# Attention in two layers: value products on four quarters of TensorE, output in two banks

## The reference

```
part 1: q, k, v = x @ w_q, x @ w_k, x @ w_v         16 heads of 64
        allowed(i, j) = same segment of 64 tokens,
                        or i - j a multiple of 4, not 0, at most 256 away
        out = softmax(q k^T / 8, allowed) v, then @ w_o
part 2: FP4 quantise-dequantise of x and weights, silu(x w_gate) * (x w_up), @ w_down (352 wide)
part 3: a gated recurrence in chunks of 64 tokens, then a silu MLP, 512 wide
part 4: sigmoid(xr W_r) * (relu(xk W_k)^2 W_v)
```

## Time and profile before

| | us |
|---|---|
| median of 3 runs (469.19, 473.04, 474.06) | 473.04 |
| span of the profiled execution, first to last instruction | 468.8 |
| TensorE busy in it (95%) | 444.4 |
| VectorE busy (84%) | 394.0 |
| ScalarE busy (71%) | 333.3 |
| GpSimd busy (63%) | 296.6 |

### The profile page before, as it was taken

How to read it: one execution, slowest core, us unless ns; L and a number is a source line. 1 busy time by engine, 2 the same in 40 slices (tenths; PEclk the granted TensorE clock), 3 DMA queues, 4 the chain that set the end, 5 groups by cost and what they waited for, 6 DMA issues and landing times.

```text
span 468.8 us, 17264 instructions
## 1 busy us (share of the span) xinstructions
PE 444.4 (95%) x6440; PEld 350.0 (75%) x6440; DVE 394.0 (84%) x1344; ACT 333.3 (71%) x975; POOL 296.6 (63%) x491
## 2 busy tenths in 40 slices
PE   7997899999999999999999999998987989999996
PEld 6685688888888888788887778887744757558775
DVE  6885798987888899889887698995899989998775
ACT  3686768868877877886786678695566579987533
POOL 4321488677666858667865588564669897674322
PEclk9999899999999999999999999999999999999999
DMA  7577852346335445344455565364000000000003
GB/s 224 183 246 209 247 142 52 73 99 133 80 74 112 76 79 105 76 85 94 98 108 124 112 124 108 75 125 91 1 1 0 0 2 1 1 0 2 1 0 91
DMA packets 136099, 40.53 MB, mean 86 GB/s; under 512 B 104977, under 2 KB 131025, under 8 KB 136017
## 3 DMA queue, kind: packets, MB, share of 16 engines
q1 hardware_dynamic: 135440, 38.38, 35.7%
q10 hardware_dynamic: 576, 1.05, 0.6%
HBM read 29.44 MB, written 9.96 MB: 84 GB/s over the span
## 4 chain that ended last, share of the span: by engine, by line
PE 59%; POOL 9%; DMA 8%; DVE 8%; ACT 7%; SPq 4%; issue 3%; ACTq 0%; POOLq 0%; DVEq 0%
PE psum L422 10%; PE psum L464 10%; PE psum L484 5%; PE psum L1186 5%; DMA w_rows_dram<-st 4%; PE psum L498 4%; PE psum L495 4%; PE psum L403 4%; PE psum L510 4%; PE psum L1181 3%; PE psum L405 3%; PE psum L404 3%; DMA st<-w_rows_dram 2%; POOL area L1827 2%; ACT pband L569 2%
## 5 line engine op out<-in xcount | busy, mean ns | idle before, releaser
L948 POOL TENSOR_SCALAR pband<-pband,fac 128x192 f32<-128x192 f32 x256 | 103.9, 424 | 80.6 <-DVE fac L771 80.4
L569 ACT ACTIVATE pband<-pband,st 128x192 f32<-128x192 f32 x256 | 113.1, 447 | 1.0 <-DVE st L719 1.0
L719 DVE CUSTOM_DVE_ANT_0 pband<-psum,band_mask 128x192 f32<-128x192 f32 x256 | 76.1, 353 | 0.1
L422 PE MATMUL psum<-keys,q_class 64*64 64x192 f32 (+2 forms) x1536 | 66.2, 274 | 0.0
L464 PEld LDWEIGHTS psum<-ident,pband 128*128 128x128 f32 x384 | 45.4, 141 | 21.4 <-issue 13.3
L422 PEld LDWEIGHTS psum<-keys,q_class 64*64 64x64 f32 x1536 | 57.6, 133 | 1.4 <-issue 1.4
L464 PE MATMUL psum<-ident,pband 128*128 128x128 f32 x384 | 53.0, 273 | 2.2 <-DVE pt L780 2.2
L569 ACT ACTIVATION_READ_ACCUMULATOR pband<-pband,st 128x1 f32 x256 | 49.3, 192 | 0.0
L938 POOL COPY q_class<-q_rows 128x512 f32<-128x512 f32 x32 | 36.5, 1142 | 19.2 <-ACT q_rows L609 19.2
L930 POOL COPY keys<-k_rows 128x512 f32<-128x512 f32 x32 | 36.1, 1130 | 14.0 <-ACT k_rows L601 7.1
L780 DVE COPY pt<-psum 128x512 f32<-128x512 f32 x64 | 43.7, 683 | 0.5
(11 more groups left out here) (213 smaller groups left out, 1090.7 us busy)
## 6 DMA issues: line engine op xcount, KB each, us to landing
v_rows_dram<-arena SPq DMA_DIRECT2D x32, 256.0 KB, 3.4
...
w_rows_dram<-st SPq DMA_DIRECT2D x64, 8.0 KB, 3.0
st<-w_rows_dram SPq DMA_DIRECT2D x64, 8.0 KB, 2.5
...
```

The costliest lines, as they stand in the source:

```text
L422: return pe.matmul(bank[2 * r + head][rows, at:at + y.shape[1]], x, y, start=True, stop=True, skip_group_check=True)
L569: act.activation(x, x, ACT.Exp, bias=mine[:, head:head + 1], scale=-1.0, accum_out=mine[:, 2 + head:3 + head]).then_inc(s_exp, 1)
L719: dve.tensor_tensor_reduce(pband[:, G % P_SLOTS, c, head, :], bank[2 * r + head][:, at:at + BAND], band_mask[:, (0, 1, 1, 2)[w], SEG * (1 ...
L948: pool.tensor_scalar(x, x, fac[:, F % 2, 1, c, head:head + 1], 1.0, ALU.mult, ALU.mult).then_inc(s_scaled, 1)
```

## The change

- **Value products.** The 64 keys of a side or segment product now lie by token half or by class parity, not by head: the rows of the array follow the keys, the columns follow the head, and so products exist for all four quarters. `out_bank` becomes two half banks (256 columns of bank 6 and of bank 7), one for each half of the window's tokens. The side products come in two calls: first those whose keys' rows and bank have the same number, then the crossed ones, after a wait for the first (`s_sides`).
- The products for b = 0 and 1 write two banks too: 16 products of 64 moving columns in place of 8 of 128.
- **Layouts.** `pband`, `pseg`, `v_seg` and `v_side` are laid out anew. The loads of `v_seg` and `v_side` keep their number; their pieces are 128 numbers (512 bytes) in place of 64.
- **Scores.** The same products in another order: for an even class the pair of products of both heads takes the same columns of the array, for an odd class the other ones.
- **Banks.** The query projection writes bank 6, the output product writes `turn_bank[0]` (bank 4). So the next projections wait for `take_out` (`s_out`), the output product waits for the even turn of the next unit to be copied out (`s_pt[0]`), and the turn for b = 0 waits for the sum of two units before (`s_acc`).
- **Order.** TensorE's step is new (below), the output product comes one step earlier, the key projection at the end of the step before. The other engines' steps, the start-up and the rest are put in a new order with the same calls.

```diff
-    s_out, s_mix, s_acc = sem("s_out"), sem("s_mix"), sem("s_acc")
+    s_sides, s_out, s_mix, s_acc = sem("s_sides"), sem("s_out"), sem("s_mix"), sem("s_acc")
 
     bank = [psum[:, k, :] for k in range(8)]
-    turn_bank, out_bank, shared_bank = bank[4:6], bank[6], bank[7]
+    turn_bank, rows_bank, shared_bank = bank[4:6], bank[6], bank[7]
+    out_bank = [bank[6 + half][:, 0:HALF_W] for half in range(2)]
+    query_bank = [shared_bank, bank[6]]
     SEG_AT = 2 * BAND
     CONST = 3
     MASKS = 15
...
     for x in range(1, FIRST_STEP):
         occupants += [(x, "key"), (x - 1, "query")]
-    occupants.append((FIRST_STEP - 1, "query"))
-    for t in range(FIRST_STEP, NS_ALL + 8):
-        occupants += [(t - lag, who) for who, lag in (("key", 0), ("wo", 7), ("query", 0)) if there(t - lag)]
+    occupants += [(FIRST_STEP - 1, "query"), (FIRST_STEP, "key")]
 
     def wait_shared(pe, x, name):
 
+        if (x, name) not in occupants:
+            pe.wait_ge(s_out, x - FIRST_STEP + (name == "query"))
+            return
         at = occupants.index((x, name))
         if at:
             pe.wait_ge(*shared_reader(*occupants[at - 1]))
...
-                    product(0, second, at, x0[:, second], y0[:, SEG:SEG + BAND])
-                    product(1, first, at, x1[:, first], y1[:, 0:BAND])
-                    product(0, first, at, x0[:, first], y0[:, SEG:BAND])
-                    product(1, second, at + SEG, x1[:, second], y1[:, SEG:BAND])
-                    product(0, first, at + P, x0[:, first], y0[:, 0:SEG])
-                    product(1, second, at, x1[:, second], y1[:, BAND:BAND + SEG])
+                    if c % 2 == 0:
+                        product(0, second, at, x0[:, second], y0[:, SEG:SEG + BAND])
+                        product(1, second, at, x1[:, second], y1[:, SEG:SEG + BAND])
+                        product(0, first, at, x0[:, first], y0[:, SEG:BAND])
+                        product(1, first, at, x1[:, first], y1[:, SEG:BAND])
+                        product(0, first, at + P, x0[:, first], y0[:, 0:SEG])
+                        product(1, first, at + P, x1[:, first], y1[:, 0:SEG])
+                    else:
+                        product(0, first, at, x0[:, first], y0[:, 0:BAND])
+                        product(1, first, at, x1[:, first], y1[:, 0:BAND])
+                        product(0, second, at + SEG, x0[:, second], y0[:, SEG:BAND])
+                        product(1, second, at + SEG, x1[:, second], y1[:, SEG:BAND])
+                        product(0, second, at, x0[:, second], y0[:, BAND:BAND + SEG])
+                        product(1, second, at, x1[:, second], y1[:, BAND:BAND + SEG])
...
                 wait(pe, s_pt[odd], e)
+                if b == 0:
+                    wait(pe, s_acc, U - 1)
...
+            def turned(U, b):
+
+                odd, e = b % 2, 2 * U + b // 2
+                pe.wait_ge(s_pt[odd], e + 1)
+                return pt[:, PT_SLOTS * odd + e % PT_SLOTS, :]
+
+            def out_by_class(half):
+                return out_bank[half].rearrange("q (x c) -> q c x", c=DIL)
+
             def weigh(U, b):
+
                 if not there(U):
                     return
                 p, w = divmod(U, NW)
-                odd, e = b % 2, 2 * U + b // 2
                 if b == 0:
+                    pe.wait_ge(s_query, min(U + FIRST_STEP, NS_ALL))
+                    pe.wait_ge(s_key, min(U + FIRST_STEP + 1, NS_ALL))
                     wait(pe, s_out, U)
                     pe.wait_ge(s_v[w], (p + 1) * V_DMAS[w])
-                if b == 2 and w < NW - 1:
-                    pe.wait_ge(s_v[w + 1], (p + 1) * V_DMAS[w + 1])
-                pe.wait_ge(s_pt[odd], e + 1)
-                turned = pt[:, PT_SLOTS * odd + e % PT_SLOTS, :]
-                by_class = out_bank.rearrange("q (x c) -> q c x", c=DIL)
-                for k in range(4):
-                    if b < 2:
-                        c, head = 2 * b + k // 2, k % 2
-                        dims = slice(DH * head, DH * (head + 1))
-                        last = pe.matmul(by_class[dims, c, :], v_both[:, c, w, dims], turned[:, P * k:P * (k + 1)],
-                                         start=(b == 0 and k < 2), stop=False, skip_group_check=True)
-                        continue
+                mine = turned(U, b)
+                for i in range(2):
+                    c = 2 * b + i
                     for half in range(2):
-                        cols = slice(P * k + SEG * half, P * k + SEG * (half + 1))
-                        side = 2 * w + 1 if half else 2 * w - 2
-                        if b == 2 and not 0 <= side < 2 * (NW - 1):
-                            continue
                         for head in range(2):
                             dims = slice(DH * head, DH * (head + 1))
-                            if b == 2:
-                                last = pe.matmul(by_class[dims, k, SEG * half:SEG * (half + 1)], v_side[dims, k, side, :],
-                                                 turned[dims, cols], start=False, stop=False, skip_group_check=True)
-                            else:
-                                last = pe.matmul(out_bank[dims, cols], v_seg[dims, 2 * (TW * w + k) + half, :],
-                                                 turned[dims, cols], start=False, stop=(k == 3 and half == 1),
-                                                 skip_group_check=True)
-                last.then_inc(s_pv[odd], 1)
+                            at = P * (2 * i + head) + SEG * half
+                            last = pe.matmul(out_by_class(half)[dims, c, :], v_both[:, c, w, dims], mine[:, at:at + SEG],
+                                             start=(c == 0), stop=False, skip_group_check=True)
+                last.then_inc(s_pv[b], 1)
+
+            def weigh_segments(U):
+
+                if not there(U):
+                    return
+                w = U % NW
+                mine = turned(U, 3)
+                for j in range(2):
+                    for second in range(2):
+                        for head in range(2):
+                            for half in range(2):
+                                dims, mykeys = slice(DH * head, DH * (head + 1)), slice(SEG * half, SEG * (half + 1))
+                                cols, at = SEG * (2 * j + second), P * (2 * j + head) + SEG * second
+                                last = pe.matmul(out_bank[half][dims, cols:cols + SEG],
+                                                 v_seg[mykeys, HALF_SEGS * w + 2 * j + second, dims],
+                                                 mine[mykeys, at:at + SEG], start=False, stop=False, skip_group_check=True)
+                last.then_inc(s_pv[1], 1)
+
+            def weigh_sides(U, crossed):
+
+
+                if not there(U):
+                    return
+                p, w = divmod(U, NW)
+                if w < NW - 1:
+                    pe.wait_ge(s_v[w + 1], (p + 1) * V_DMAS[w + 1])
+                mine = turned(U, 2)
+                if crossed:
+
+                    pe.wait_ge(s_sides, U + 1)
+                for d in range(2):
+                    for head in range(2):
+                        for odd in range(2):
+                            half = odd ^ crossed
+                            side = 2 * w + 1 if half else 2 * w - 2
+                            if not 0 <= side < 2 * (NW - 1):
+                                continue
+                            dims, mykeys = slice(DH * head, DH * (head + 1)), slice(SEG * odd, SEG * (odd + 1))
+                            at = P * (2 * d + head) + SEG * half
+                            last = pe.matmul(out_by_class(half)[dims, 2 * d + odd, :], v_side[mykeys, d, side, dims],
+                                             mine[mykeys, at:at + SEG], start=False, stop=False, skip_group_check=True)
+                last.then_inc(s_pv[0] if crossed else s_sides, 1)
 
             def output(U):
                 if not there(U):
                     return
                 if U == 0:
                     pe.wait_ge(s_wo, 16)
-                wait_shared(pe, U, "wo")
+                pe.wait_ge(s_pt[0], min(2 * (U + 2), 2 * NS_ALL))
+                wait(pe, s_acc, U)
                 pe.wait_ge(s_out, U + 1)
-                pe.matmul(shared_bank[:, :], wo[:, U // NW, :], o_sb[:, :], start=True, stop=True).then_inc(s_mix, 1)
+                pe.matmul(turn_bank[0][:, :], wo[:, U // NW, :], o_sb[:, :], start=True, stop=True).then_inc(s_mix, 1)
 
             pe.wait_ge(s_con, 2)
             pe.wait_ge(s_const, CONST)
...
             for t in range(FIRST_STEP, DRAIN):
-                project(t, 1)
                 weigh(t - 6, 0)
                 weigh(t - 6, 1)
-                turn(t - 6, 3)
-                output(t - 7)
+                scores(t - 2, 0)
+                weigh_segments(t - 6)
+                weigh_sides(t - 6, 0)
+                scores(t - 2, 1)
+                weigh_sides(t - 6, 1)
```

(23 more changed lines are left out.)

272 lines of the change are left out of this document (140 added, 132 removed).

## The result

| | before | after |
|---|---|---|
| median of the runs, us | 472.1 | 483.2 |
| profiled execution's span | 468.8 | 483.9 |
| first copy into `o_sb` | 66.5 | 69.1 |
| last copy into `o_sb` | 341.9 | 340.4 |
| from it to the end | 126.9 | 143.5 |

The change makes the kernel slower: ratio 1.025, 95% interval 1.020 to 1.031. The forecast was 456 us. The profiled execution of the kernel after is the longest of its four (485.86 us, the others 480.1 to 483.9), so stretches read from its trace are at the upper end.

What follows compares the result with a forecast made beforehand. TensorE, never idle over 20 attention steps of 9.0 us, was taken as the bound. Steps -12.1, late and following steps -0.6 and -1.6, last units -1.5, start-up -1, parts 2 to 4 0: 473.0 - 16.8 = 456.2 us, range 449 to 466.

Steps and rivals of the forecast that it cites:

- parts 2 to 4: The kernel's parts after attention: the same work in another order, put at 0 us (+3 to -3).
- the step as a whole: Each of the 20 attention steps with its waits: 8.4 us, so 168.0 against 180.1, -12.1.
- the late steps: Three steps after the 20, held by statistics round trips and SyncE's queue: -0.6 us; three loop steps after them: -1.6.
- The step of TensorE alone: TensorE's own work in an attention step: middle step 9.27 to 8.30 us, edge step 8.79 to 8.28.
- Rivals 2 and 3: 2: segment products no faster on four quarters, 471 us, chance 0.08; 3: class products keep 54 ns per record, 478, 0.05.
- rival 2: Value products: four quarters not twice as fast, 471 us, chance 0.08; by the 25 ns rule middle step 8.9, about 467.
- The second circle: Attention step: key projection, ScalarE's exponentials, VectorE's factors and even-turn copy, a turn, key projection again: 8.36 us.
- Rival 1: Attention loop: circles of waits between TensorE, ScalarE and VectorE close at 8.75 us, not 8.4: 465 us, chance 0.17.
- The last five units: Five units in the hand-written rest win their value products partly: -1.5 us (0 to -3).
- Start-up: The 66.5 us before the first copy into `o_sb`: one more key projection, fewer packets, -1 us (+1 to -3).
- rival 4: More gain than forecast: late steps follow TensorE, parts 2 to 4 gain 3 us by new order: 449 us, chance 0.06.
- sign that it was wrong altogether: A start-up or a rest that is longer by more than 3 us.

Runs made afterwards that it cites:

- half_products: The changed kernel with half of the side products and half of the segment products left out: 481.9 us, ratio 1.021 to the kernel before.
- best: The changed kernel with the edits of `last_bank` and `rows_on_act` together: 470.1 us, ratio 1.001 to the kernel before.
- last_bank: The changed kernel with parts 2 to 4 in the old order and the last unit's output product in bank 7, not 4: 475.9 us, ratio 1.007.
- rows_on_act: The changed kernel with eleven loads (part 2's rows, plain weights) issued by ScalarE instead of SyncE: 477.7 us, ratio 1.012 to the kernel before.

## Why the prediction was wrong

Three of its terms failed: parts 2 to 4, put at nothing (point 6, over half of the miss), the step as a whole (2) and the late steps (3).

1. *The step of TensorE alone, 8.3.* Right as far as the runs show: segments 14 ns, classes 30 ns apart; without pauses (176.3 - 9.5) / 20 = 8.34. Rivals 2 and 3 are out. (By the rule in rival 2 a middle step comes to 8.30 + 2 x 0.35 = 9.0, not 8.9.) The second circle, put at 8.36, was right too, as `half_products` shows (8.39), so a shorter TensorE step alone would have won nothing more. The rule of the Trainium skill ("TensorE: Matmul & The Clock Gate", "Wait — 56ns, not 53.3ns?"), matmuls never less than about 25 ns apart, doesn't hold for four quarters: the row has 14.
2. *The step as a whole, 8.4.* Wrong, 8.8. The failed step is the sum of TensorE's step from records of a kernel in which no pause occurs: it has no term for the supply of instructions. The change puts 3833 records into 176.3 us where there were 3512 in 180.1, and crowds them, the fastest 124 into 2.2 us instead of 3.1; the seams of the instruction packets then cost 0.48 a step. Rival 1 had the length of the step (8.75), but not the cause: of the waits that it named, the one for `take_out` comes once (1.4 us) and the one for VectorE's copy twice (0.7 us), and taking away the waits for the statistics, or some of VectorE's work, changed nothing.
3. *Late steps and loop steps after them, -2.2.* Wrong, +2.8 in the profiled execution (from -0.3 to +4.6 in the five kernels with the same loop). I had seen SyncE's round of 10.5 us and still counted on some gain. The round is a circle of its own, 10.5 us before and 11.2 after, and doesn't follow TensorE. Eleven issues moved to ScalarE bring 4.2 us (`best` against `last_bank`) to 6.8. A stretch of 6.8 us at the lower clock, which the kernel before doesn't have, adds to the 2.8.
4. *The last five units, -1.5.* Measured -3.1.
5. *Start-up, -1.* Measured +2.6, but it varies from 63.9 to 70.2 in kernels with the same start-up; no cause was tested.
6. *Parts 2 to 4, 0 (±3).* Wrong by 16.6, half of all, and the step that decided the sign. "The same work in another order" was costed at nothing, without a row that shows what an order costs. It costs 11.6 by itself on the old attention. I even counted it as a gain in rival 4. Of the waits that it makes, those for `y(0)` and `hb` were seen; moving `y(0)` won nothing, so which waits carry the 11.6 stays open. The prediction's own sign that it was wrong altogether, a rest longer by more than 3 us, is what came.
7. *The sign.* The gain in attention was real, 1.5 us at the last copy, and 10.2 (331.7) in `rows_on_act`; it never reached the forecast 16.8, and the rest ate it.
